# Expert tiles of 256 rows with stationary weights, loaded and split per tile, in a convolution, attention and mixture-of-experts kernel

## The reference

```
x = x + conv(groupnorm(x))      # 3x3 block DCT, 192x192 product, exact gelu, inverse DCT
t = t + attn(layernorm(t))      # per image of 256 tokens; inside: layernorm, z = silu(n Wqk + b),
                                # v, gate = silu(n Whid + b); A = relu(q k^T / 256)^2; (A v * gate) Wout + x
t = t + moe(layernorm(t))       # router: top 2 of 8 experts, softmax of the two logits
                                # expert e: gelu(u Wi[e]^T + bi[e]) Wo[e]^T + bo[e];  192 -> 768 -> 192
```

## Time and profile before

| | |
|---|---|
| median of 3 runs | 761.24 us (760.74 to 767.37) |
| the profiled execution's own time | 759.72 us |
| its span, first to last instruction | 757.9 us |
| busy share of the span: TensorE, its weight loads | 91%, 82% |
| VectorE, ScalarE, GpSimd | 61%, 44%, 34% |
| mean granted TensorE clock, as a share of full | 0.974 |

### The profile page before, as it was taken

The page is one execution under the profiler, slowest core; times in us unless marked ns, Lnnn a source line. Parts: engine busy times, 40 slices in busy tenths (PEclk is TensorE's granted clock), DMA queues, the critical chain, the costliest instruction groups (busy, mean ns, idle before and its releaser), DMA issues.

```text
span 757.9 us, 16610 instructions
## 1 busy us (share of the span) xinstructions
PE 691.6 (91%) x4136; PEld 619.3 (82%) x4137; DVE 465.8 (61%) x1718; ACT 335.1 (44%) x500; POOL 259.9 (34%) x250
## 2 busy tenths in 40 slices
PE   3987886899999999994799999999999999999993
PEld 3876776788878788882699999998999998999893
DVE  5788988667777787777445454454545444454541
ACT  2433334566666667561343443433344343333330
POOL 3544554105343443434232232322223232322322
PEclk9999999999999999997799999999999999999997
DMA  8211111002121211112622222222222222222221
GB/s 270 87 47 47 31 49 42 12 11 80 47 73 52 68 57 44 72 43 89 179 36 37 42 31 42 36 37 36 37 41 32 42 36 37 36 37 41 32 31 16
DMA packets 32570, 40.08 MB, mean 53 GB/s; under 512 B 4853, under 2 KB 27990, under 8 KB 32424
## 3 DMA queue, kind: packets, MB, share of 16 engines
q1 hardware_dynamic: 18566, 25.98, 12.0%
q0 software_dynamic: 13296, 13.35, 11.6%
q10 hardware_dynamic: 690, 0.55, 0.3%
HBM read 22.38 MB, written 17.47 MB: 53 GB/s over the span
## 4 chain that ended last, share of the span: by engine, by line
DMA 33%; issue 10%; DVE 5%; PE 1%; SPq 1%; DVEq 1%; POOLq 0%; POOL 0%; ACT 0%
DMA out_rows<-y_sb,y_id 32%; DVE y_sb L1017 3%; DVE y_id L1014 1%; PE ps L1034 1%; DVE y_sb L1012 1%; DMA slot_rows<-lists 1%; DVEq L1012 1%; SPq L424 0%; POOLq L606 0%; DVEq L1017 0%; SPq L425 0%; SPq L486 0%; POOL out_rows L603 0%; SPq L487 0%; SPq L497 0%
## 5 line engine op out<-in xcount | busy, mean ns | idle before, releaser
L603 POOL DMA_INDIRECT out_rows<-y_sb,y_id x71 | 110.8, 1560 | 273.4 <-DVE y_sb L1017 260.0
L1034 PE MATMUL ps<-w_o_sb,hT 128*128 x852 | 158.2, 336 | 10.1 <-DVE hT L1022 6.1
L1034 PEld LDWEIGHTS ps<-w_o_sb,hT 128*128 128x128 f32 x852 | 137.7, 191 | 26.8 <-issue 26.8
L700 ACT ACTIVATE h_sb<-ps 128x768 f32<-128x768 f32 x71 | 57.5, 810 | 224.0 <-PE ps L1034 224.0
L1012 DVE TENSOR_TENSOR y_sb<-ps,b_o_sb 128x192 f32<-128x192 f32 x71 | 25.4, 358 | 170.8 <-DMA out_rows<-y_sb,y_id 165.2
L1034 PE MATMUL ps<-w_hi,sT_hi 96*128 (+1 forms) x284 | 103.8, 365 | 1.3 <-DVE sT_lo L1000 1.3
L1034 PE MATMUL ps<-w_hi,sT_lo 96*128 (+1 forms) x284 | 97.5, 343 | 0.0
L1034 PE MATMUL ps<-w_lo,sT_hi 96*128 (+1 forms) x284 | 97.0, 342 | 0.0
L700 ACT ACT_TABLE_LOAD x71 | 91.1, 1283 | 6.4 <-issue 5.1
L1022 DVE COPY hT<-ps 128x384 f32<-128x384 f32 x142 | 72.1, 550 | 1.4 <-PE ps L1236 1.4
L1236 PE MATMUL ps<-const,h_sb 128*128 128x128 f32 x426 | 58.2, 273 | 1.9 <-ACT h_sb L700 1.9
(11 more groups left out here) (192 smaller groups left out, 1308.8 us busy)
## 6 DMA issues: line engine op xcount, KB each, us to landing
slot_rows<-lists SPq DMA_DIRECT2D x71, 97.0 KB, 2.1
w_o_sb<-in_w_o SPq DMA_DIRECT2D x8, 576.0 KB
out_rows<-w_o_sb SPq DMA_DIRECT2D x16, 192.0 KB, 1.8
h_sb<-in_split_w SPq DMA_DIRECT2D x9, 288.0 KB
hT<-in_split_w SPq DMA_DIRECT2D x9, 288.0 KB
w_o_sb<-in_x SPq DMA_DIRECT2D x1, 1536.0 KB, 12.3
out_rows<-y_sb,y_id POOLq DMA_INDIRECT x71, 3.5
w_o_sb<-in_x SPq DMA_DIRECT2D x1, 768.0 KB, 9.0
```

What stands on the lines that cost most here:

```text
L603: pool.indirect_dma_start(out=out, out_offset=bass.IndirectOffsetOnAxis(ap=y_id[:, 0:1], axis=0), in_=y_sb[:, :], in_offset=None, compute_ ...
L700: act.activation(h_sb[:, :].rearrange("p (b n) -> p b n", b=2), ps_h, ACT.Gelu).then_inc(h_done, 1)
L1034: return pe.matmul(dst, lhsT, rhs, start=start, stop=stop)
```

## The change

- The tile loop works on 31 tiles of 256 rows (pairs) and 9 of 128 rows (singles). Pairs come first; a table for each kind is made (three in all).
- W_i is no longer kept split in SBUF. SP loads the expert's W_i for each tile (128x1536 float32, two buffers); ScalarE casts the high part in two instructions, VectorE subtracts the low part in two.
- In the W_i product the weights are stationary and the rows move, so h comes out transposed and its transposes and copies go. The bias b_i enters as the gelu's bias.
- The 192 channels are held as a block of 128 and one of 64; the second block holds the high part of its 64 channels in rows 0 to 63 and the low part in rows 64 to 127 of one tile, against the weights twice. So five passes do what six did, in the attention too. The bias of W_hidden and W_qk goes in with extra rows of the pass with 97 rows.
- Rows are turned by `turn_rows`: two transposes and a float32 product with the identity for 128 rows.
- The router logits come out with tokens on partitions at once, without logitsT.
- X, v, gate, sim and gated get SBUF of their own; all of W_o is loaded ahead of the attention; in the convolution only W_hidden is split, in one instruction on each engine.
- Scatters: y_sb has two buffers; GpSimd launches two scatters for a pair and doesn't wait for their landing. VectorE waits for it, now after the add of b_o.

```diff
+        we_in = sb("we_in", [P, 2, 2 * FF])
+        we_hi = sb("we_hi", [P, 2, 2 * FF], f32r)
+        we_lo = sb("we_lo", [P, 2, 2 * FF], f32r)
+        hid_in = we_in[:, 0, :].rearrange("p (k f) -> p k f", k=2)
+        b_hid_sb, b_hid_hi = (we_in[0:KBB, 1, n * SLICE:(n + 1) * SLICE] for n in range(2))
+        b_i_sb = sb("b_i_sb", [P, EXPERTS * FCHUNKS])
...
+            def load_weights(j, odd):
+                e = sp.value_load(tile_expert[0:1, ds(j, 1)], min_val=0, max_val=EXPERTS - 1)
+                sp.dma_start(we_in[:, odd, :].unsqueeze(1), w_i[:, ds(e, 1), :]).then_inc(we_in_done[odd], 16)
             def load_tile(j, odd):
                 at = sp.value_load(tile_row[0:1, ds(j, 1)], min_val=0, max_val=SPARE)
-                sp.dma_start(slot_rows[:, odd, :], lists[ds(at, P), :]).then_inc(rows_in[odd], 16)
+                n = rows_of(j)
+                sp.dma_start(slot_rows[:, odd, 0:n, :],
+                             lists[ds(at, n * P), :].rearrange("(p t) c -> p t c", t=n)).then_inc(rows_in[odd], 16)
...
             def load_next(j, odd):
+                wait_alone(sp, we_done, j - 1, ld_const)
+                load_weights(j, odd)
                 wait_alone(sp, sT_ps, j - 1, ld_const)
                 sp.wait_ge(meta_done, j - 1)
                 load_tile(j, odd)
...
+                if isinstance(i, int) and i == 1:
+                    pool.wait_ge(hi_done, 1)
+                    pool.tensor_tensor(w_lo[:, :, :], hid_in, w_hi[:, :, :].bitcast(f32),
+                                       ALU.subtract).then_inc(parts_done, 1)
...
+            pool.wait_ge(bias_hi_done, 1)
+            lo = slice(BIAS_LO, BIAS_LO + 1)
+            pool.tensor_tensor(w_lo[lo, 1, :], b_hid_sb[lo, :], b_hid_hi[lo, :], ALU.subtract)
+            pool.tensor_tensor(w_qk_lo[lo, 1, :], b_qk_sb[lo, :], b_qk_hi[lo, :], ALU.subtract).then_inc(bias_done, 1)
...
+            def add_rows(j, odd, nth):
+                wait_alone(pool, y_done[odd], nth, ld_const)
+                for t in range(rows_of(j)):
+                    pool.indirect_dma_start(
+                        out=out, out_offset=bass.IndirectOffsetOnAxis(ap=y_id[:, odd, t:t + 1], axis=0),
+                        in_=y_sb[:, odd, t, :], in_offset=None, compute_op=ALU.add).then_inc(added, 16)
...
+                    act.wait_ge(ld_hid, 16)
+                    act.activation(w_hi[:, :, :], hid_in, ACT.Copy).then_inc(hi_done, 1)
...
+            act.activation(w_lo[hi, 1, :], b_hid_sb[hi, :], ACT.Copy)
+            act.activation(w_qk_lo[hi, 1, :], b_qk_sb[hi, :], ACT.Copy)
+            act.activation(b_hid_hi[lo, :].bitcast(f32r), b_hid_sb[lo, :], ACT.Copy)
+            act.activation(b_qk_hi[lo, :].bitcast(f32r), b_qk_sb[lo, :], ACT.Copy).then_inc(bias_hi_done, 1)
...
+                    act.activation(nB_bias[0:KB, :], ps_nT[0:KB, 1, :], ACT.Identity, bias=ln_sb[0:KB, 1, 1:2],
+                                   scale=ln_sb[0:KB, 0, 1:2]).then_inc(nB_bias_done, 1)
...
+            def moe_step(j, odd):
+                if not absent(j + 1, MOE_TILES):
+                    act.wait_ge(we_in_done[1 - odd], (j + odd) * 8 + 16)
+                    wait(act, h_ps, j * (FCHUNKS // 2))
+                    for k in range(2):
+                        here = slice(k * FF, (k + 1) * FF)
+                        act.activation(we_hi[:, 1 - odd, here], we_in[:, 1 - odd, here], ACT.Copy).then_inc(we_hi_done, 1)
+                if not absent(j, MOE_TILES):
+                    n = rows_of(j) * P
+                    if isinstance(j, int) and j == FIRST_TILES:
+                        act.wait_ge(tiles_done, 6)
+                    e = act.value_load(tile_expert[0:1, ds(j, 1)], min_val=0, max_val=EXPERTS - 1)
+                    for b in range(FCHUNKS // 2):
+                        act.wait_ge(h_ps, j * (FCHUNKS // 2) + b + 1)
+                        for c in range(2):
+                            f = 2 * b + c
+                            last = act.activation(hT[:, odd, f, 0:n].unsqueeze(1), ps_h[:, b, c, 0:n].unsqueeze(1),
+                                                  ACT.Gelu, bias=b_i_sb[:, ds(e * FCHUNKS + f, 1)])
+                        last.then_inc(h_done, 1)
+                if not absent(j + 1, MOE_TILES):
+                    n = rows_of(j + 1) * P
+                    act.wait_ge(sT_ps, j + 2)
+                    act.activation(sA_hi[:, 0:n], ps_sT[:, 0, 0:n], ACT.Copy)
+                    act.activation(sB[:, 0:n], ps_sT[:, 1, 0:n], ACT.Copy).then_inc(sT_hi_done, 1)
+            pipeline(act, moe_step, **MOE)
...
             def moe_step(j, odd):
                 if not absent(j + 1, MOE_TILES):
-                    dve.wait_ge(sT_ps, j + 2)
-                    dve.tensor_copy(sT_hi[0:KC, :, :], ps_sT).then_inc(sT_hi_done, 1)
+                    for k in range(2):
+                        here = slice(k * FF, (k + 1) * FF)
+                        wait_alone(dve, we_hi_done, 2 * j + 3 + k, ld_const)
+                        last = dve.tensor_tensor(we_lo[:, 1 - odd, here], we_in[:, 1 - odd, here],
+                                                 we_hi[:, 1 - odd, here].bitcast(f32), ALU.subtract)
+                    last.then_inc(we_done, 1)
+                if not absent(j + 1, MOE_TILES):
+                    n = rows_of(j + 1)
                     wait_alone(dve, sT_hi_done, j + 2, ld_const)
-                    dve.tensor_tensor(sT_lo[0:KC, :, :], ps_sT, sT_hi[0:KC, :, :].bitcast(f32),
+                    dve.tensor_tensor(sA_lo[:, 0:n * P], ps_sT[:, 0, 0:n * P], sA_hi[:, 0:n * P].bitcast(f32),
+                                      ALU.subtract)
+                    dve.tensor_tensor(sB[KB:P, 0:n * P], ps_sT[KB:P, 1, 0:n * P], sB[KB:P, 0:n * P].bitcast(f32),
                                       ALU.subtract).then_inc(sT_done, 1)
-                    dve.tensor_copy(meta[:, ds(j + 1, 1), :],
-                                    slot_rows[:, 1 - odd, D:D + 2].bitcast(i32).unsqueeze(1)).then_inc(meta_done, 1)
+                    dve.tensor_copy(meta[:, ds(j + 1, 1), 0:n, :],
+                                    slot_rows[:, 1 - odd, 0:n, D:D + 2].bitcast(i32).unsqueeze(1)).then_inc(meta_done, 1)
                 if isinstance(j, int) and j == -1:
-                    make_table(list_at[:, :], list_first[:, :], 0, FIRST_TILES)
+                    make_table(list_at[:, :], list_first[:, :], P, FIRST_TILES, TWO, 1)
+                    after_pairs(single_first[:, :], list_first[:, :], PAIRS)
+                    make_table(list_at[:, :], single_first[:, :], 0, 0, P, 2)
                 if not absent(j - 1, MOE_TILES):
                     p = j - 1
+                    n = rows_of(p)
                     e = dve.value_load(tile_expert[0:1, ds(p, 1)], min_val=0, max_val=EXPERTS - 1)
                     dve.wait_ge(y_ps, p + 1)
-                    wait(dve, added, p * 16)
-                    dve.tensor_tensor(y_sb[:, :].unsqueeze(1), ps_y.unsqueeze(1), b_o_sb[:, ds(e, 1), :],
+                    here = y_sb[:, 1 - odd, 0:n, :]
+                    dve.tensor_tensor(here, ps_y[:, 0:n, :], b_o_sb[:, ds(e, 1), :].broadcast_to((P, n, D)),
                                       ALU.add).then_inc(y_read, 1)
-                    dve.tensor_copy(y_id[:, :].unsqueeze(1), meta[:, ds(p, 1), 0:1])
-                    dve.wait_ge(y_read, p + 1)
-                    w = meta[:, ds(p, 1), 1:2].bitcast(f32)
-                    dve.tensor_scalar(y_sb[:, :], y_sb[:, :], w.rearrange("p a b -> p (a b)"), None,
-                                      ALU.mult).then_inc(y_done, 1)
-                if not absent(j, MOE_TILES):
-                    for k in range(2):
-                        dve.wait_ge(hT_ps, 2 * j + 1 + k)
-                        dve.tensor_copy(hT[:, k * FF // 2:(k + 1) * FF // 2], ps_hT[:, k, :]).then_inc(hT_done, 1)
+                    wait_alone(dve, y_read, p + 1, ld_const)
+                    wait(dve, added, added_before(p))
+                    dve.tensor_copy(y_id[:, 1 - odd, 0:n].unsqueeze(1), meta[:, ds(p, 1), 0:n, 0])
+                    for t in range(n):
+                        w = meta[:, ds(p, 1), t, 1:2].bitcast(f32)
+                        last = dve.tensor_scalar(y_sb[:, 1 - odd, t, :], y_sb[:, 1 - odd, t, :],
+                                                 w.rearrange("p a b -> p (a b)"), None, ALU.mult)
+                    last.then_inc(y_done[1 - odd], 1)
                 if isinstance(j, int) and j == 0:
+                    dve.wait_ge(table_ps, 2)
...
+            def turn_rows(dst, rows, here):
+                pe.transpose(dst[:, 0, here], rows[:, 0:KA], K("ident"))
+                pe.transpose(dst[0:KB, 1, here], rows[:, KA:D], K("ident"))
+                return mm(dst[KB:P, 1, here], rows[:, KA:D], K("ident"))
...
+            def products(dst, hi, lo, columns, n_first, at=slice(0, SEQ)):
```

(63 more changed lines are left out.)

365 lines of the change are left out of this document (168 added, 197 removed).

## The result

| | before | after |
|---|---|---|
| median | 761.68 us | 801.3 us (796.5 to 802.9, 4 runs) |
| ratio, 95% interval | | 1.049 (1.043 to 1.056) |
| profiled execution: own time, span | 759.72, 757.9 | 800.44, 798.6 |
| granted TensorE clock | 0.974 | 0.946 |

The change makes the kernel 40 us slower; the forecast was 694. One execution of experiment 2 ran at a lower granted clock than the other (0.942 for 0.961) and took longer; no comparison uses it. The stage table, the same columns as the earlier trace rows, shows which part of the span carries it.

A forecast was written before the change was run, and what follows sets the result against it. The tile loop was taken as paced by the scatter ring, with TensorE within 0.3 us. Convolution -15, attention -10, tile loop -49.5, its start +9 sum to -65.5 on 759.7: 694 us, range 682 to 706 (668 to 730 without far ends).

The forecast's parts named there:

- The 64-row pass: Tile loop, W_i products of a pair: 30 passes at 0.12 each, 3.6 us, or 5.7 if loads were not overlapped.
- The slots: Tile loop, slot turns: two transposes and two fp32 passes per half, 0.85 us a pair.
- first four terms: Convolution: steady steps -14, first images -2, scale instructions -3, the whole W_hidden split +2 us.
- the other -8: Between convolution and first table: bias rows ahead of the attention +2, attention images -10 us.
- Singles: Tile loop, tiles of 128 rows: 5.6 us a step (5.1 to 7.5), against 5.26 before.
- The start: From tables to first W_o product: later casts, split and second table, +9 us (3 to 15), 1 of it half clock.
- Rival 2: Tile loop: scatter ring, stretched by W_i's load bursts, sets the pair step at 9.4 to 10.5, 710 to 744 us; chance 0.16.
- Rival 5: Tile loop: weights not stationary long enough, 0.19 a W_i pass, 2.1 us more a pair, 759 us; chance 0.02.
- Rival 3: Tile loop: slower than before, ring with bursts and held launches in full, pairs and singles, up to 793 us; chance 0.04.
- The convolution: Without w_lo subtractions stalling VectorE, steps fall from 6.86 to 5.75 us; sum -15 including bias rows, bounds -24 to -4.
- The attention: Five passes for six and new turns and logits: -0.65 us an image, -10 over 16, bounds -15 to 0.
- Table loads: Tile loop, ScalarE: the old loop's 71 table loads were expected gone.

The follow-up runs named there:

- experiment 2: The changed kernel with the order of passes turned round in odd chunks, so two 64-row passes stand side by side: 751.4 and 763.0 us.
- experiment 1: The changed kernel with the 64-row low-part pass of W_i taken with all 128 rows: 735.1 us, ratio 0.965.
- experiment 5: experiment 3 plus SyncE issuing a tile's W_i load only after scatters of tiles four and more before landed: 660.5 us, ratio 0.867.
- experiment 3: experiment 1 with row turns as three transposes, without the product written at partition 64: 728.6 us, 715.8 on another chip.
- experiment 4: experiment 1 with an unused GpSimd subtraction of 97x768 put back in every convolution step: 755.9 us in one run.

## Why the prediction was wrong

- *The 64-row pass: the step that failed.* "The gates load weights of the same width at 0.12, so 3.6." The gates' passes of the earlier trace rows have 96 and 97 rows; one in five of the new ones has 64. The forecast gave all 30 one price, 0.12 with the loads beside the passes or 0.19 without (3.6 or 5.7 a pair); the term measured 5.95. With experiments 1 and 2 the cost is shown to be 0.37 to 0.38 for each visit to 64 rows, 2.28 a pair, 71 us in 31 pairs. In y_id copies: 31 pair steps took 346.9 for 275.9.
- *The slots.* 0.85 forecast, 1.41 measured, the same kind of hole. The same turns in the attention cost an image 0.7 more than without the part at partition 64 (12.8 against 12.14). In the mean an image takes 12.9 for the 12.57 forecast, as from the tenth on they are longer. The -23.6 does not show it: the last step of the convolution ends 16.7 earlier (99.41 for 116.12) for the 17 of the forecast's first four terms, and from there to the first table it is -6.9 for the other -8. What made up there for the images isn't taken apart.
- *Singles.* 8.67 a step for 5.6, 24.6 us in eight. At full clock a single takes 7.77 (760.98 to 768.75), and 6.05 in experiment 1: the visits cost 1.7 of the 3.1, 0.28 each at 128 columns. The passes start 0.11 apart, not the 0.095 of the transposes, which is 0.45 more. The other 0.9 comes with the clock, 0.74 from 700 to 740 us, by turns full and half while TensorE is busy throughout. In experiment 5 a single takes 5.58, with clock 0.99. What drops the clock in the change isn't shown.
- *The start.* +18 for +9. TensorE idles until 347.8 and stays at the half clock until after 356 us, so that the first pair's W_i products take 10.1 for 5.95; I had put 1 us on it. That is 4 of the 9; the rest isn't taken apart. The windows after the tables, columns as in the earlier trace rows:

```profile
344.00:350.00 6.00, 2.18 (x7) 1.76 (x8) 4.61 (x16) 3.58 (x6) 1.52 (x2) 0.50 0.48 130
350.00:356.00 6.00, 6.00 (x20) 4.21 (x18) 4.89 (x19) 2.96 (x5) 0.00 (x0) 0.50 0.31 123
```

- *Rival 2, the ring stretched by W_i's bursts,* was right as a mechanism and, with 9.4 to 10.5, in its size: 9.9 in the mean of experiments 1 and 3. In the change it is hidden by a slower TensorE. I named the place, beside the second scatter; my ground against it, that the launch is ahead of need, does not hold, as the load is issued in the same instant.
- *Rival 5* had the right place and nearly the right size (759 with 0.19 a pass, which is 5.7), and half the mechanism: it had the loads beside no pass. Between passes of 128 rows they do lie beside them, 0.11 apart; at each visit two loads do not (453.54 and 453.85 above). It needed to be held against each form of the new passes, not against all. That its size comes near the measured pair (5.7 for 5.95) is luck.
- *Rival 3,* the slow side, I had given to the ring; the time came from TensorE. The shared ports, which the forecast calls its second rival, are in this third one.
- *The convolution* was right, and by its reason: experiment 4 puts 17 us back there with the subtraction alone. The 6.86 that the forecast started from is the shorter of two steps that alternate, 7.12 in the mean, so the saving is 1.34 a step for its 1.1. *The attention's* early images take 12.8 for the 12.57 forecast. *Table loads* went, as expected: 4 are left in the kernel.

## What to carry to other kernels

List the row and column extents of each TensorE instruction of a new inner loop, and not only their number and width: a pass that holds 64 rows between passes of 128 cost 0.37 us here and saved nothing, and padding it (or placing two side by side) is one edit. Where a ring through DMA is near the engine's own step, look at what is issued in the instant in which the ring's transfer starts; a wait that moves a load by a few microseconds was worth 55 us here, but only after TensorE's step was below the ring's. Two limits, one under the other, are told apart by removing the upper one first, and by running each fix alone and together on one chip.

## What was not expected of the hardware

- A visit of TensorE to a 64-row pass between 128-row passes costs 0.37 to 0.38 us more than its 0.11 at 256 columns and 0.28 more at 128, 240 times in this kernel. The weight loads on both sides of it don't lie beside a pass. Three turns of which one writes 64 columns at partition 64 take 0.68 (457.94 to 458.62), three without such a one 0.33 in experiment 3.
- A scatter with addition that starts together with a load of 786 KB lands in 5.2 to 7.0 us (the change, experiments 1 and 3); in 3.5 in the median when that load is 8 KB.
- Of the launches on GpSimd that lie beside VectorE's two-input splits of W_i, a third last 1.91 for 1.56 (13 of 37 in the change), the others 1.56 to 1.65; of the 34 that don't, none is over 1.6. That is 0.35 of the 0 to 1.8 allowed for in the forecast.
- In some executions every second of the later images of the attention took up to 1.7 us longer, in others of the same kernel none did (experiment 3, one profile on each of two chips).
